# Two fused layers on one core: later sweeps' weights worked out in quads 1 to 12, and the second layer's low halves of weights moved from GpSimd to VectorE

## The chip, the core and the metric

The kernel runs on one core of a Trainium2 chip. Its engines are TensorE (PE in the profile, with its weight loads as PEld), VectorE (DVE), ScalarE (ACT), GpSimd (POOL) and SyncE (SP, which here only issues DMAs). The metric is the device time of one execution in microseconds. The kernel before takes 2681.8 us, the median of three runs (2679.82 to 2686.71).

## The reference, cut to what matters

Two layers follow each other on x of 32 x 128 x 2048 in float32. Layer 0 mixes the 128 channels of each batch by a matrix of its own (a softmax over 8 experts, from a small MLP) and then applies a 2048 x 2048 linear layer whose weight has a low-rank sum added to it. Layer 1 is a grouped convolution of 9 taps and then, on permuted columns, 16 heads of 128 -> 512 -> gelu -> 128. Each layer adds its result to its input.

```
x = x + (einsum('bsd,od->bso', cond(x), W) + bias + einsum('ebsr,eor,e->bso', xa, Bf, coeffs*scales))
t = conv(x)[:, perm]; t = gelu(einsum('bhd,hdm->bhm', t, up)); t = einsum('bhm,hmd->bhd', t, down)
x = x + t[:, unperm]
```

All is float32. The kernel gets that from TensorE's fp32r type by splitting each operand into a high half (a copy rounded to fp32r, `ACT.Copy`) and a low half (the operand minus the high half, one `tensor_tensor` subtract), and by three matmuls: high x high, high x low, low x high.

## The kernel before, in words

**Layer 0.** Two blocks of code follow each other, `layer0_block` and `layer1_block`, with a barrier between them. In the opening of layer 0 the full weight (W plus the low-rank part) is made in 32 tiles, and part of it is stored to `weff_d` in HBM. Then come 32 quads. A quad takes four batches and one quarter of the weight, and does 14 items: 7 products of a Strassen-like scheme for each of two pairs of batches (p = 0, 1). An item is 12 matmuls of 128x512, so a quad is 168 product matmuls (line 478). Eight quads make a sweep, and each sweep uses its own quarter of the weight: `tw_hi` and `tw_lo`, seven matrices of 128x2048 each. Quads 16 to 31 are the final ones: they add the halves of quads 0 to 15, apply the mixing of channels (`mix_v`, 24 more matmuls a quad, line 496), and put the result into x1.

Each engine runs one list of instructions that is written out by `quads(slot, ...)`: for quad q and item t, `slot(q, t)` says what stands there. ScalarE splits off the high half of the left operand three items ahead (`split`, line 611), VectorE the low half (line 952). Four ring buffers hold them, so TensorE has about three items of lead. GpSimd makes the sums of the scheme (lines 789 to 807). In the final quads VectorE also takes results out of PSUM (line 999), splits `v` (line 1011) and applies `take_mixed` (line 1026), and GpSimd issues the accumulating DMAs of the result (line 816).

**The weights of sweeps 1 to 3** need four of the seven matrices as sums of blocks. That is done in 24 pieces, 8 for a sweep. For piece n, SP loads 2 x 256 KB from `weff_d` into `mix` (`load_mix`, line 374) once the store of piece n - 1 has landed, GpSimd adds the blocks to a running sum (lines 309, 311) and makes the four differences (lines 826 to 832), and ScalarE's queue stores `mix` to `t_d` (`store_mix`). There is one `mix` buffer. `mixes(q)` says which pieces a quad does: two in each of quads 1 to 4 (for sweep 1), 9 to 12 (sweep 2) and 17 to 20 (sweep 3). Half a quad before a sweep starts, ScalarE's queue begins to load the seven matrices of 1 MB (`load_tw`), ScalarE splits them (line 701) and VectorE makes their low halves in 28 instructions (line 1031), from item 7 of the sweep's last quad to item 6 of the next.

**Weights of layer 1.** They are 32 chunks of 128x512 (up and down of 16 heads). 16 early chunks go through in layer 0's last quad, two at each of items 6 to 13 (`freed_chunks`): loaded by SP (`load_early`), high half on ScalarE (line 706), low half on GpSimd (`split_early`, line 860). The other 16 go through in layer 1's lead.

**The lead of layer 1** is 20 steps before the first head. In each step u TensorE does the convolution of one unit (9 matmuls, line 1446) and four transposes (line 1458), ScalarE splits the next unit and takes the convolution out, and VectorE makes the low half (line 1599) and takes the transposes (line 1619). SP loads four pieces of each unit (line 88), loads chunks n + 4 and n + 5 after chunks n and n + 1 are split (`load_weights`, line 1266; there are four stage buffers), and after each fourth unit stores four pieces of z (`store_z`, line 1314). The chunks have two of steps 4 to 11 each: high half on ScalarE (line 1512), low half on GpSimd (`split_weights`, line 1377). After the store of the fourth batch GpSimd gathers the first head (line 1371), and TensorE starts `up` (line 1421). From there the two layers' rest, 1080 us, is untouched.

Of the kernel before, what the change touches and what calls it, by code (L numbers as in the profile page):

```python
# [7 lines left out]
ALU = mybir.AluOpType  # L8
# [31 lines left out]
QUADS = 32  # L40
FINAL = QUADS // 2
EARLY = 16
ITEMS = 14
# [69 lines left out]
def sweep(q):  # L113
    return q // 8
# [30 lines left out]
def layer0_block(nc, sh, x, x_t, cond_w, bias_k, cond_t, w0, b0, w1, b1, w2, b2, w_t, bias, lora_a, lora_b, coeffs, scales,  # L145
# [4 lines left out]
    with ExitStack() as ctx:  # L150
# [105 lines left out]
        def freed_chunks(q, t):  # L256

            n = 2 * (ITEMS * (q - QUADS + 1) + t - 6)
            return range(n, n + 2) if 0 <= n < EARLY else ()

# [16 lines left out]
        def mixes(q):  # L277

            return ((q % 8 - 1, 0), (q % 8 - 1, 1)) if 1 <= q % 8 <= 4 and q < 24 else ()

        def mix_count(q):
            return 8 * sweep(q) + 2 * (q % 8 - 1)

# [14 lines left out]

        def sum_piece(eng, engine, q, c):

            n = mix_count(q) + c
            half = HALVES[sweep(q) + 1][0]
            total = sums[half].rearrange("p (b n) -> p b n", b=2)[:, :, c * 256:(c + 1) * 256]
            top, low = mix[:, 0:2, :], mix[:, 2:4, :]
            if q == 1:
                engine.tensor_tensor(total, top, low, ALU.add).then_inc(sums_ready, 1)
            else:
                eng.wait_ge(sums_ready, sums_count(n - 1))
                engine.tensor_tensor(total, total, top, ALU.add).then_inc(sums_ready, 1)
                eng.wait_ge(sums_ready, sums_count(n) - 1)  # L310
                engine.tensor_tensor(total, total, low, ALU.add).then_inc(sums_ready, 1)

        @block.sync
        def _(sp):
# [47 lines left out]

            def load_mix(q, i, c):
                oh, dh = HALVES[sweep(q) + 1]
                n = mix_count(q) + c
                if n == 0:
# [36 lines left out]
            def slot(q, t):  # L403
# [13 lines left out]
                if mixes(q) and t in (0, 7):  # L417
                    load_mix(q, *mixes(q)[t // 7])
# [152 lines left out]
        def _(act):  # L571
# [135 lines left out]

            def store_mix(q, i, c):
                act.wait_ge(t_ready, 16 + 4 * (mix_count(q) + c + 1))
                act.dma_start(t_d[sweep(q), i, :, :, c * 256:(c + 1) * 256], mix[:]).then_inc(mix_out, 16)  # L710

            def slot(q, t):
# [30 lines left out]
                if mixes(q) and t in (6, 12):  # L743
                    store_mix(q, *mixes(q)[t // 12])

# [3 lines left out]
        def _(pool):  # L749
# [67 lines left out]

            def mix_piece(q, c):
                n = mix_count(q) + c
# [3 lines left out]
                sum_piece(pool, nc.gpsimd, q, c)  # L823
                pool.wait_ge(sums_ready, sums_count(n))
# [32 lines left out]

            def split_early(n):
                pool.wait_ge(sh.wsplit_hi, n + 1)
                nc.gpsimd.tensor_tensor(tw_lo[n // 4][:, n % 4, :], w_stage[n % 5], fp32(tw_hi[n // 4][:, n % 4, :]),  # L860
                                        ALU.subtract).then_inc(sh.wsplit_lo, 1)

            def slot(q, t):
# [12 lines left out]
                if mixes(q) and t in (2, 9):  # L876
                    mix_piece(q, t // 9)
# [5 lines left out]
                for n in freed_chunks(q, t):  # L883
                    split_early(n)

# [3 lines left out]
        def _(dve):  # L889
# [123 lines left out]
            def take_mixed(n):  # L1013
# [26 lines left out]
            def slot(q, t):  # L1040
# [12 lines left out]
                for n in range(8 * FINAL, 8 * QUADS):  # L1053
                    if mix_slot(n) + 2 == ITEMS * q + t:
                        take_mixed(n)
                for n in range(1, 4):
                    at = ITEMS * (q - 8 * n + 1) + t - 7
# [11 lines left out]
def layer1_block(nc, sh, x1_d, up, down, perm, ident, z_d, y_d, out):  # L1069

    with ExitStack() as ctx:
# [282 lines left out]
        def _(pool):  # L1354
# [19 lines left out]

            def split_weights(n):
                pool.wait_ge(wsplit_hi, G + n + 1)
                nc.gpsimd.tensor_tensor(chunk(w_lo, n), stage[n % 4], fp32(chunk(w_hi, n)),  # L1377
                                        ALU.subtract).then_inc(wsplit_lo, 1)

            def step(k, h, parity):  # L1380
                if lead(k):
                    for n in chunks_of(k, h):
                        split_weights(n)
                if exists(k, h, 2) and not ahead(k, h):
# [201 lines left out]
        def _(dve):  # L1586
            def split_kernel(g):
# [169 lines left out]
```

## Time and profile before

| | |
|---|---|
| median of 3 runs | 2681.8 us (2679.82 to 2686.71) |
| profiled execution | 2675.54 us, of which its span is 2673.7 us |
| opening of layer 0 | to 117.0 us, the first product matmul |
| quads 0 to 31 | 117.0 to 1507 us |
| end of layer 0 to the first convolution | 1507 to 1526.6 us |
| lead of layer 1 | 1526.6 to 1593.6 us |
| heads of layer 1 | 1593.6 to 2673.7 us |

Quad q starts with the (168 q + 1)-th product matmul. Quads 1 to 7 and 9 to 15 last 38.9 to 39.2 us each, quads 21 to 23 and 25 to 30 last 44.5 to 45.0 us each (they have 24 matmuls more). The others differ: quad 0 lasts 41.8, quad 8 42.5, quad 16 50.9, quads 17 to 20 53.6, 51.1, 51.8 and 50.4, quad 24 52.2, quad 31 48.9 us (to its last product matmul).

### The profile page before, as it was taken

How to read it: one execution, taken by the hardware profiler on the slowest of the kernel's cores; microseconds unless marked ns; L12 is line 12 of the kernel's file. 1: busy time of each engine (PE TensorE's matmuls, PEld its weight loads, DVE VectorE, ACT ScalarE, POOL GpSimd, SP SyncE). 2: the span in 40 equal slices, each digit the busy share in tenths (PEclk: the TensorE clock that was granted, in tenths of full speed). 3: DMA queues.
4: the chain of work that ended last, by engine and by line, in shares of the span. 5: the costliest groups of instructions: out<-in, count | busy, mean ns of one | idle time of the engine just before them, and what ended most of it. 6: DMA issues, size and time to landing. Idle time of an engine off the chain costs nothing. (4 is left out here: it accounts for less than half of the span.)

```text
span 2673.7 us, 38662 instructions
## 1 busy us (share of the span) xinstructions
PE 2558.8 (96%) x11458; PEld 2070.2 (77%) x11458; DVE 2089.7 (78%) x2847; ACT 1143.8 (43%) x1905; POOL 1025.4 (38%) x879
## 2 busy tenths in 40 slices
PE   7899999999999989999999789999999999999997
PEld 6678887888877768878888568888888888888775
DVE  6766767776688788897878658888888888888776
ACT  3233334333342223343333355555555555555563
POOL 4545632674236463344434432222222222222231
PEclk9999999999999999999999899999999999999998
DMA  8887769887776776867676764476767776777686
GB/s 292 285 275 261 259 221 306 267 279 251 237 250 148 179 183 133 224 162 171 138 161 136 157 187 137 138 220 205 231 203 225 212 223 212 222 220 219 191 270 242
DMA packets 437718, 570.38 MB, mean 213 GB/s; under 512 B 38280, under 2 KB 263872, under 8 KB 437504
## 3 DMA queue, kind: packets, MB, share of 16 engines
q1 hardware_dynamic: 329552, 345.68, 42.8%
q0 software_dynamic: 39840, 101.45, 17.3%
q10 hardware_dynamic: 68112, 120.69, 12.8%
q8 instruction: 98, 1.61, 0.3%
q14 instruction: 116, 0.95, 0.1%
HBM read 339.08 MB, written 228.59 MB: 212 GB/s over the span
## 5 line engine op out<-in xcount | busy, mean ns | idle before, releaser
L478 PE MATMUL ps_c<-w_hi,ring_hi 128*128 128x512 f32 x1792 | 711.0, 397 | 6.6 <-DVE ring_lo L952 6.5
L478 PE MATMUL ps_c<-w_hi,ring_lo 128*128 128x512 f32 x1792 | 709.3, 396 | 0.0
L478 PE MATMUL ps_c<-w_lo,ring_hi 128*128 128x512 f32 x1792 | 708.3, 395 | 0.0
L952 DVE TENSOR_TENSOR ring_lo<-raw_n,ring_hi 128x512 fp32r<-128x512 f32 x384 | 447.8, 1169 | 196.2 <-ACT ring_hi L611 184.9
L611 ACT ACTIVATE ring_hi<-raw_n 128x512 fp32r<-128x512 f32 x384 | 243.0, 634 | 758.3 <-PE ps_c L478 503.0
L1403 POOL DMA_INDIRECT y_d<-y_s,idx x128 | 147.1, 1149 | 737.7 <-ACT y_s L1574 680.4
L1541 ACT ACTIVATE kern<-ps_up 128x512 f32<-128x512 f32 x512 | 306.2, 598 | 261.3 <-PE ps_up L1421 233.3
L478 PEld LDWEIGHTS ps_c<-w_hi,ring_hi 128*128 128x128 f32 x1792 | 338.3, 189 | 91.5 <-DVE ring_lo L952 11.6
L478 PEld LDWEIGHTS ps_c<-w_lo,ring_hi 128*128 128x128 f32 x1792 | 338.5, 189 | 79.8 <-issue 0.5
L478 PEld LDWEIGHTS ps_c<-w_hi,ring_lo 128*128 128x128 f32 x1792 | 338.1, 189 | 79.4
L1649 DVE TENSOR_TENSOR g_lo<-kern,g_hi 128x512 fp32r<-128x512 f32 x512 | 354.7, 693 | 40.8 <-ACT g_hi L1545 23.4
L1644 DVE CAST g_hi<-kern 128x512 fp32r<-128x512 f32 x474 | 202.6, 427 | 87.2 <-ACT kern L1541 84.8
L1431 PE MATMUL ps_y<-g_hi,w_hi 128*128 128x512 f32 x512 | 213.5, 417 | 7.0 <-ACT y_s L1574 7.0
L999 DVE TENSOR_TENSOR r_early<-ps_c,r_early 128x512 f32<-128x512 f32 x192 | 131.5, 685 | 100.4 <-PE ps_c L478 99.9
L1431 PE MATMUL ps_y<-g_hi,w_lo 128*128 128x512 f32 x512 | 201.8, 394 | 0.0
L1431 PE MATMUL ps_y<-g_lo,w_hi 128*128 128x512 f32 x512 | 200.9, 392 | 0.0
L1421 PE MATMUL ps_up<-t_hi,w_hi 128*128 128x512 f32 x472 | 187.0, 396 | 7.1 <-DVE t_lo L1608 7.1
L1421 PE MATMUL ps_up<-t_hi,w_lo 128*128 128x512 f32 x472 | 185.8, 394 | 0.0
L1421 PE MATMUL ps_up<-t_lo,w_hi 128*128 128x512 f32 x472 | 184.1, 390 | 0.0
L789 POOL TENSOR_TENSOR s<-raw_n 128x512 f32<-128x512 f32 x64 | 88.8, 1415 | 207.3 <-DMA raw_n<-in_x_t 199.6
L1446 PE MATMUL ps_c<-xp_hi,cw_hi 128*128 128x512 f32 x354 | 142.3, 402 | 17.1 <-DVE xp_lo L1599 17.0
L1558 ACT ACTIVATE z_s<-ps_c,cbias 128x512 f32<-128x512 f32 x118 | 81.1, 688 | 173.5 <-PE ps_c L1446 107.5
(224 smaller groups left out, 4334.2 us busy)
## 6 DMA issues: line engine op xcount, KB each, us to landing
raw_n<-in_x_t SPq DMA_DIRECT2D x128, 512.0 KB, 6.0
u_s<-x_d SPq DMA_DIRECT2D x496, 64.0 KB, 2.2
z_d<-x_s SPq DMA_DIRECT2D x120, 256.0 KB
rear<-y_d SPq DMA_DIRECT2D x112, 256.0 KB
rear<-x_d SPq DMA_DIRECT2D x112, 256.0 KB
out_dram<-results SPq DMA_DIRECT2D x112, 256.0 KB
u_s<-in_x SPq DMA_DIRECT2D x64, 256.0 KB, 5.5
half_d<-r_early ACTq DMA_DIRECT2D x64, 256.0 KB, 4.1
```

The source lines that it names most:

```text
L478: mm = nc.tensor.matmul(bank, a[:, dc, :], w[k][:, dc, :], start=(first and dc == 0 and n == 0), stop=(dc == 3 and n == 2), skip_group_che ...
L611: nc.scalar.activation(ring_hi[g % RING][:].rearrange("p a n -> p (a n)"), ring_raw[p][k], ACT.Copy).then_inc(hi_ready, 1)
L789: nc.gpsimd.tensor_tensor(s1[:, p, :], a21, a22, ALU.add).then_inc(s_ready, 1)
L952: nc.vector.tensor_tensor(ring_lo[g % RING][:].rearrange("p a n -> p (a n)"), ring_raw[p][k], fp32(ring_hi[g % RING][:].rearrange("p a n - ...
L999: nc.vector.tensor_tensor(r_s[p][blk], bank, r_s[p][blk], ALU.add).then_inc(read, 1)
L1403: nc.gpsimd.indirect_dma_start(out=y_d[parity], out_offset=bass.IndirectOffsetOnAxis(ap=idx[:, h:h + 1], axis=0), in_=y_s[j][:], in_offset ...
L1421: mm = nc.tensor.matmul(ps_up[:, mc, :], chunk(w, 2 * h)[:, mc * P:(mc + 1) * P], t, start=(n == 0), stop=(n == 2))
L1431: mm = nc.tensor.matmul(ps_y[:, 0, :], chunk(w, 2 * h + 1)[:, mc * P:(mc + 1) * P], g[:, mc, :], start=(mc == 0 and w is w_hi and g is g_h ...
L1446: mm = nc.tensor.matmul(acc, w[:, 3 * g + tau, :], x[:, tau:tau + Q], start=(tau == 0 and n == 0), stop=(tau == 2 and n == 2))
L1541: nc.scalar.activation(g_s[:, mc, :], ps_up[:, mc, :], ACT.Gelu).then_inc(gelu_done, 1)
L1644: nc.vector.tensor_copy(g_hi[:, mc, :], g_s[:, mc, :]).then_inc(ghi_ready, 1)
L1649: nc.vector.tensor_tensor(g_lo[:, mc, :], g_s[:, mc, :], fp32(g_hi[:, mc, :]), ALU.subtract).then_inc(glo_ready, 1)
```

## The change

`mixes(q)` now gives pieces 2q - 2 and 2q - 1 for each of quads 1 to 12, so that all 24 pieces are done by quad 12, eight quads before the last was done. `EARLY` falls from 16 to 8: eight early chunks pass in layer 0's last quad, one at each of items 6 to 13, and their low halves are made by VectorE. The 24 others pass in the lead of layer 1, two in each of steps 4 to 15, and their low halves are made by VectorE too. The number of instructions of each kind of work is the same; 32 subtractions of 128x512 leave GpSimd for VectorE.

```diff
-EARLY = 16
+EARLY = 8
...
         def freed_chunks(q, t):
 
-            n = 2 * (ITEMS * (q - QUADS + 1) + t - 6)
-            return range(n, n + 2) if 0 <= n < EARLY else ()
+            n = ITEMS * (q - QUADS + 1) + t - 6
+            return range(n, n + 1) if 0 <= n < EARLY else ()
...
         def mixes(q):
 
-            return ((q % 8 - 1, 0), (q % 8 - 1, 1)) if 1 <= q % 8 <= 4 and q < 24 else ()
-
-        def mix_count(q):
-            return 8 * sweep(q) + 2 * (q % 8 - 1)
+            return (2 * q - 2, 2 * q - 1) if 1 <= q <= 12 else ()
...
-            half = HALVES[sweep(q) + 1][0]
+            half, c = HALVES[n // 8 + 1][0], n % 2
...
                 for n in range(EARLY if q == QUADS - 1 else 0):
-                    if t == ((5, 5, 5, 6, 7)[n] if n < 5 else 7 + (n - 4) // 2):
+                    if t == ((5, 5, 5, 6, 7)[n] if n < 5 else 3 + n):
                         load_early(n)
...
+            def split_early(n):
+                dve.wait_ge(sh.wsplit_hi, n + 1)
+                nc.vector.tensor_tensor(tw_lo[n // 4][:, n % 4, :], w_stage[n % 5], fp32(tw_hi[n // 4][:, n % 4, :]),
+                                        ALU.subtract).then_inc(sh.wsplit_lo, 1)
...
+            def split_weights(n):
+                dve.wait_ge(wsplit_hi, G + n + 1)
+                nc.vector.tensor_tensor(chunk(w_lo, n), stage[n % 4], fp32(chunk(w_hi, n)),
+                                        ALU.subtract).then_inc(wsplit_lo, 1)
...
                 if lead(k):
                     split_x(*after(k, h))
+                    for n in chunks_of(k, h):
+                        split_weights(n)
```

Three places in the order of instructions. First GpSimd, from the end of quad 4 through quad 5 into quad 6; `s` and `raw_n` are the sums of the scheme, `kern` and `mix` a piece. Before:

```order
L832 TENSOR_TENSOR mix<-mix 128x256
L789 TENSOR_TENSOR s<-raw_n 128x512 x2
L795 TENSOR_TENSOR raw_n<-raw_n 128x512 x2
L801 TENSOR_TENSOR raw_n<-s,raw_n 128x512 x2
L807 TENSOR_TENSOR raw_n<-raw_n 128x512 x2
L789 TENSOR_TENSOR s<-raw_n 128x512 x2
```

Now:

```order
L827 TENSOR_TENSOR mix<-mix 128x256
L785 TENSOR_TENSOR s<-raw_n 128x512 x2
L791 TENSOR_TENSOR raw_n<-raw_n 128x512 x2
L797 TENSOR_TENSOR raw_n<-s,raw_n 128x512 x2
L803 TENSOR_TENSOR raw_n<-raw_n 128x512 x2
L305 TENSOR_TENSOR kern<-kern,mix 128x2x256
L307 TENSOR_TENSOR kern<-kern,mix 128x2x256
L821 TENSOR_TENSOR mix<-mix 128x256
L823 TENSOR_TENSOR mix<-mix 128x256
L825 TENSOR_TENSOR mix<-mix 128x256
L827 TENSOR_TENSOR mix<-mix 128x256
```

The piece of six instructions stands behind the four pairs of sums, twice in each of quads 5 to 8, and no longer in quads 17 to 20.

Second SP's queue around the start of quad 8, where the sweep changes: `raw_n` are the left operands of quad 8, `u_s` and `x_n` the pieces of x to which the bias is added. Before:

```order
L332 DMA raw_n<-in_x_t 128x1024
L357 DMA u_s<-in_x 128x512
L332 DMA raw_n<-in_x_t 128x1024 x2
L357 DMA x_n<-in_x 128x512 x2
L357 DMA u_s<-in_x 128x512 x2
L346 DMA x_n<-in_bias 128x1024
```

Now:

```order
L370 DMA mix<-weff_d 128x2x256 x2
L328 DMA raw_n<-in_x_t 128x1024
L353 DMA u_s<-in_x 128x512
L328 DMA raw_n<-in_x_t 128x1024
L353 DMA u_s<-in_x 128x512
L328 DMA raw_n<-in_x_t 128x1024 x2
L353 DMA x_n<-in_x 128x512 x2
L370 DMA mix<-weff_d 128x2x256 x2
L353 DMA u_s<-in_x 128x512 x2
L342 DMA x_n<-in_bias 128x1024
```

A pair of `mix` loads stands ahead of quad 8's left operands, and another at quad 8's start, ahead of the loads of x.

Third VectorE in the lead, steps 4 to 6: `g_lo` and `xp_lo` are the low half of a unit, `x_s` and `rear` the transposes taken. Before:

```order
L1599 TENSOR_TENSOR g_lo<-u_s,g_hi 128x514
L1619 COPY x_s<-ps_zt 128x16x32
L1599 TENSOR_TENSOR xp_lo<-u_s,xp_hi 128x514
L1619 COPY rear<-ps_zt 128x16x32
L1599 TENSOR_TENSOR g_lo<-results,g_hi 128x514
```

Now:

```order
L1591 TENSOR_TENSOR g_lo<-u_s,g_hi 128x514
L1583 TENSOR_TENSOR w_lo<-kern,w_hi 128x512 x2
L1611 COPY x_s<-ps_zt 128x16x32
L1591 TENSOR_TENSOR xp_lo<-u_s,xp_hi 128x514
L1583 TENSOR_TENSOR w_lo<-kern,w_hi 128x512 x2
L1611 COPY rear<-ps_zt 128x16x32
L1591 TENSOR_TENSOR g_lo<-results,g_hi 128x514
```

Two subtractions of weights stand between a unit's low half and the taking of the transposes, in 12 steps.

## Rows read from the trace of the kernel before

**Rows 1.** The page, part 1: busy us (share of the span) xinstructions.
```profile
PE 2558.8 (96%) x11458; PEld 2070.2 (77%) x11458; DVE 2089.7 (78%) x2847; ACT 1143.8 (43%) x1905; POOL 1025.4 (38%) x879
```

**Rows 2.** Stretches: quad 6, quad 10, quads 17 to 20, quads 21 and 22.
```profile
core 0: us, PE busy (x) PEld busy (x) DVE busy (x) ACT busy (x) POOL busy (x), PEclk, DMA share, GB/s
353.50:392.40 38.90, 38.90 (x169) 31.55 (x168) 21.13 (x28) 12.50 (x22) 10.31 (x8) 1.00 0.65 202
512.90:551.80 38.90, 38.90 (x169) 31.55 (x168) 28.53 (x29) 12.75 (x22) 26.83 (x21) 1.00 0.83 272
797.70:1004.60 206.90, 186.45 (x770) 148.42 (x769) 173.37 (x182) 54.72 (x92) 122.64 (x113) 0.96 0.71 165
1004.60:1093.60 89.00, 89.00 (x385) 72.10 (x384) 73.39 (x89) 27.39 (x46) 36.90 (x32) 1.00 0.71 148
```

**Rows 3.** Groups of VectorE, quads 17 to 20: count, busy us, mean ns, idle before.
```profile
L952 DVE TENSOR_TENSOR ring_lo<-raw_n,ring_hi 128x512 fp32r<-128x512 f32 x48 | 80.4, 1674 | 8.5 <-ACT ring_hi L611 7.7
```

**Rows 4.** The same of quads 21 and 22.
```profile
L952 DVE TENSOR_TENSOR ring_lo<-raw_n,ring_hi 128x512 fp32r<-128x512 f32 x24 | 30.4, 1269 | 2.0 <-ACT ring_hi L611 1.4
```

**Rows 5.** Timeline in quad 17: start us, us, engine, line, op, tiles [idle before <-releaser].
```profile
804.12 3.77 DVE L952 TENSOR_TENSOR ring_lo<-raw_n,ring_hi 128x512 fp32r<-128x512 f32 x1
...
805.75 1.57 POOL L309 TENSOR_TENSOR kern<-kern,mix 128x512 f32<-128x512 f32 x1
...
809.62 0.50 PE L496 MATMUL ps_v<-v_hi,agg_hi 128*128 128x512 f32 x1 [2.04 <-DVE v_lo L1011]
```

**Rows 6.** Stretches: end of quad 7, start and end of quad 8.
```profile
411.90:431.40 19.50, 19.50 (x85) 15.78 (x84) 13.02 (x19) 9.32 (x13) 4.61 (x4) 1.00 1.03 369
431.40:452.00 20.60, 18.08 (x75) 13.49 (x74) 20.60 (x27) 12.81 (x15) 7.12 (x5) 1.00 0.96 329
452.00:473.90 21.90, 21.90 (x96) 17.75 (x95) 14.89 (x22) 7.07 (x13) 5.56 (x5) 1.00 0.78 261
```

**Rows 7.** DMA issues in quad 2: queue, count, KB each, median us to landing.
```profile
mix<-weff_d SPq DMA_DIRECT2D x4, 256.0 KB, 3.8
...
t_d<-mix ACTq DMA_DIRECT2D x2, 512.0 KB, 3.4
```

**Rows 8.** Waits, 410 to 475 us: engine line <- releaser: total us, times, longest.
```profile
ACT ring_hi L611 <- DMA raw_n<-in_x_t: 12.3, 4, 7.0
```

**Rows 9.** Stretches: quads 30 and 31.
```profile
1413.70:1458.10 44.40, 44.40 (x193) 36.03 (x192) 38.56 (x46) 13.69 (x23) 17.86 (x16) 1.00 0.72 149
1458.10:1507.00 48.90, 44.89 (x192) 35.72 (x191) 43.46 (x44) 22.07 (x37) 30.80 (x27) 1.00 0.67 151
```

**Rows 10.** Groups of VectorE in quad 31.
```profile
L952 DVE TENSOR_TENSOR ring_lo<-raw_n,ring_hi 128x512 fp32r<-128x512 f32 x9 | 15.8, 1758 | 0.8 <-ACT ring_hi L611 0.6
L1011 DVE TENSOR_TENSOR v_lo<-r_early,v_hi 128x512 fp32r<-128x512 f32 x4 | 8.2, 2062 | 0.0
...
L1004 DVE TENSOR_TENSOR agg_lo<-agg,agg_hi 128x512 fp32r<-128x512 f32 x1 | 0.7, 684 | 0.0
```

**Rows 11.** Timeline in quad 31.
```profile
1497.39 6.21 DVE L1011 TENSOR_TENSOR v_lo<-r_early,v_hi 128x512 fp32r<-128x512 f32 x1
...
1503.65 0.50 PE L496 MATMUL ps_v<-v_hi,agg_hi 128*128 128x512 f32 x1 [3.61 <-DVE v_lo L1011]
```

**Rows 12.** SP's own waits, 1525 to 1600 us.
```profile
SPq L1266 <- POOL w_lo L1377: 3.1, 4, 1.6
```

**Rows 13.** Timeline in the lead, 1548 to 1560 us.
```profile
1555.56 1.39 ACT L1512 ACTIVATE w_hi<-kern 128x512 fp32r<-128x512 f32 x2 [4.75 <-DMA kern<-in_up]
```

**Rows 14.** Chain that ended last, in the lead: start us, us, what.
```profile
1568.77 0.42 SPq L88
1569.23 0.42 SPq L88
...
1581.75 0.52 SPq L1314
...
1593.60 1.63 PE ps_up L1421 x3
```

More of the change, by code:

```diff
@@ L297, in sums_count, with sum_piece @@
             return 9 + n if n < 2 else 8 + 2 * n
-        def sum_piece(eng, engine, q, c):
-            n = mix_count(q) + c
-            half = HALVES[sweep(q) + 1][0]
+        def sum_piece(eng, engine, n):
+            half, c = HALVES[n // 8 + 1][0], n % 2
             total = sums[half].rearrange("p (b n) -> p b n", b=2)[:, :, c * 256:(c + 1) * 256]
             top, low = mix[:, 0:2, :], mix[:, 2:4, :]
-            if q == 1:
+            if n < 2:
                 engine.tensor_tensor(total, top, low, ALU.add).then_inc(sums_ready, 1)
@@ L361, in load_r, with load_mix @@
                 sp.dma_start(r_s[p][blk], half_sum(q, p, blk)).then_inc(r_in[p][blk], 16)
-            def load_mix(q, i, c):
-                oh, dh = HALVES[sweep(q) + 1]
-                n = mix_count(q) + c
+            def load_mix(n):
+                oh, dh = HALVES[n // 8 + 1]
+                i, c = n % 8 // 2, n % 2
                 if n == 0:
@@ L417, in slot @@
                 if mixes(q) and t in (0, 7):
-                    load_mix(q, *mixes(q)[t // 7])
+                    load_mix(mixes(q)[t // 7])
                 for n in biased_at(q, t, 0):
@@ L706, in split_early, with store_mix @@
                 nc.scalar.activation(tw_hi[n // 4][:, n % 4, :], w_stage[n % 5], ACT.Copy).then_inc(sh.wsplit_hi, 1)
-            def store_mix(q, i, c):
-                act.wait_ge(t_ready, 16 + 4 * (mix_count(q) + c + 1))
-                act.dma_start(t_d[sweep(q), i, :, :, c * 256:(c + 1) * 256], mix[:]).then_inc(mix_out, 16)
+            def store_mix(n):
+                act.wait_ge(t_ready, 16 + 4 * (n + 1))
+                act.dma_start(t_d[n // 8, n % 8 // 2, :, :, n % 2 * 256:(n % 2 + 1) * 256], mix[:]).then_inc(mix_out, 16)
             def slot(q, t):
@@ L743, in slot @@
                 if mixes(q) and t in (6, 12):
-                    store_mix(q, *mixes(q)[t // 12])
+                    store_mix(mixes(q)[t // 12])
             quads(slot, -3)
@@ L816, in store_mixed, with mix_piece @@
                 pool.dma_start(piece(x1_d, n), res[n % 4], accum_op=ALU.add).then_inc(sh.res_out[n % 4], 16)
-            def mix_piece(q, c):
-                n = mix_count(q) + c
+            def mix_piece(n):
                 pool.wait_ge(mix_in, 32 * (n + 1))
@@ L822, in mix_piece @@
                     pool.wait_ge(twlo_ready, 28)
-                sum_piece(pool, nc.gpsimd, q, c)
+                sum_piece(pool, nc.gpsimd, n)
                 pool.wait_ge(sums_ready, sums_count(n))
@@ L856, in prepare_layer1 @@
                                    conv_w[:, :, kr * GC:(kr + n) * GC]).then_inc(sh.cw_in, 16)
[L858 to L861, printed above, removed]
             def slot(q, t):
@@ L876, in slot @@
                 if mixes(q) and t in (2, 9):
-                    mix_piece(q, t // 9)
+                    mix_piece(mixes(q)[t // 9])
                 for n in range(8 * FINAL, 8 * QUADS):
@@ L882, in slot @@
                     prepare_layer1(q - 24)
-                for n in freed_chunks(q, t):
-                    split_early(n)
             quads(slot, -4)
@@ L1055, in slot @@
                         take_mixed(n)
+                for n in freed_chunks(q, t):
+                    split_early(n)
                 for n in range(1, 4):
@@ L1373, in gather @@
                     in_offset=bass.IndirectOffsetOnAxis(ap=idx[:, h:h + 1], axis=0)).then_inc(t_in[j], 16)
[L1375 to L1378, printed above, removed]
             def step(k, h, parity):
-                if lead(k):
-                    for n in chunks_of(k, h):
-                        split_weights(n)
                 if exists(k, h, 2) and not ahead(k, h):
```

## The prediction

> **What bounds the kernel now.** I read the page's busy times first, and then cut the span into quads, because a share over two unlike layers says little. TensorE is busy 96% of the span, VectorE 78%, GpSimd 38% [rows 1], so time can be won only where TensorE's matmuls stand apart. The view by stretches shows where. In quads 6, 10, 21 and 22 TensorE is busy for the whole stretch; in quads 17 to 20 it is busy for 186.45 of 206.90 us [rows 2]. These four are final quads with the same number of matmuls as quads 21 and 22, which take 89.00 us for two. What they have besides is GpSimd: 122.64 us of work in four quads, against 36.90 us in two [rows 2].
>
> How GpSimd reaches TensorE is seen in VectorE's rows. The subtraction of two operands from SBUF that feeds the ring takes 1269 ns in quads 21 and 22 and 1674 ns in quads 17 to 20 [rows 3, 4]. In the timeline one of them lasts 3.77 us, from 804.12 us on, and spans an addition of a piece on GpSimd that starts at 805.75; TensorE then stands still 2.04 us for a low half of v [rows 5]. VectorE is late by GpSimd's work, and in a final quad it has little room: 73.39 us busy of 89.00 even without pieces [rows 2]. In quad 10 two pieces also run (GpSimd 26.83 us against 10.31 in quad 6), VectorE is busy 28.53 of 38.90 us, and TensorE loses nothing [rows 2]. So a piece costs time in a final quad and none in an early one, unless that quad is itself short of VectorE. One is: at the start of quad 8, where VectorE splits a new sweep's weights, it is busy 20.60 of 20.60 us [rows 6].
>
> **Quads 17 to 20: -28.9 us.** The eight pieces leave. The four quads become like quads 21 and 22: 206.9 - 2 x 89.0 = 28.9 us, or 3.6 us for a piece. Only VectorE's delay goes; what is late next is nothing that shows in quads 21 and 22, whose matmuls stand back to back. The half-speed stretches behind those stalls (the granted clock is 0.96 in the mean there, 1.00 after) are inside the 28.9. I leave quads 16 and 24 as they are, since no piece lay in them.
>
> **Quads 5 to 8: +6.0 us.** The eight pieces arrive in early quads. In 5, 6 and the first half of 7 I cost them at nothing: quad 10 is the row for that, and what hides them is VectorE's 10.4 us of idle time there and TensorE's lead of three items, which is 3 x 12 x 0.232 = 8.4 us (38.9 us over 168 matmuls is 0.232). The second piece of quad 7 and the first of quad 8 meet the change of sweep. There two things are full. The DMA engines show a share of 1.03 at 369 GB/s from 411.9 to 431.4 us, and 0.96 after it [rows 6]; ScalarE already waits for left operands around it, 12.3 us in four times, the longest 7.0 [rows 8]. VectorE has no idle time at the start of quad 8, and TensorE is busy 18.08 of these 20.60 us [rows 6].
> A piece moves 2 x 256 KB in and 512 KB out, 1 MB [rows 7]. Of this the load of the piece at quad 7's item 7 and part of the store before it, about 0.9 MB, go ahead of quad 8's left operands: 0.9 MB at 369 GB/s is 2.4 us later for operands whose slack is already used up. To it comes the first piece of quad 8, beside a full VectorE, at the 3.6 us of the final quads, together 6.0 us. The ends: nothing, if it is hidden as in quad 10; and 6.2 + 5.4 = 11.6 us if VectorE stands still for all of GpSimd's work in a piece ((122.64 - 2 x 36.90) / 8 = 6.1 us, taken as 6.2 with the gaps) and 2 MB are in the way. SP's queue counts here too: it waits at quad 8's start until the store of the piece before has landed, and the loads of x for the bias are behind that wait. In the trace these loads wait for other stores anyway, so I add nothing, but it is inside the upper end.
> A VectorE subtraction of 3.77 us spans a whole GpSimd addition of 1.57 us [rows 5]. The Trainium skill (SBUF — State Buffer, "Who interferes with whom") says that a VectorE instruction with two SBUF inputs contends with a GpSimd instruction that reads SBUF, and that the one which starts first holds the ports for its whole length while the other fully blocks. By that rule the piece in quad 8 costs about its whole 6.2 us and the sum below is 2.6 us less of a gain; by quads 17 to 20 it costs 3.6, because instructions that read PSUM slip between, and I go by these. Full blocking is in the second rival.
>
> **Quad 31: -4.5 us.** Quad 31 takes 48.9 us and quad 30 44.4, with the same matmuls [rows 9]. In it GpSimd makes 16 low halves (30.80 us busy against 17.86), and VectorE's instructions swell: four subtractions of v take 2062 ns each, one of them 6.21 us, and TensorE waits 3.61 us for it [rows 10, 11]. Now GpSimd makes none. VectorE gets eight more, at the 0.68 us of an undisturbed one [rows 10], 5.5 us. It gives back more than that: nine ring subtractions at 1758 instead of 1269 ns [rows 4, 10] and four of v at 2062 instead of 684 are 4.4 + 5.5 = 9.9 us. So it would be busy 43.5 - 9.9 + 5.5 = 39.1 of 44.4 us, as in quad 30 (38.56). Each new one stands last in its item, behind which is the next item's take out of PSUM; its high half was made by ScalarE earlier in the same item. Ends: -4.5 and, if the eight fall on TensorE's waits for v, -4.5 + 5.5 = +1.0.
>
> **The lead: +2.4 us.** The chain that ended last runs here over SP's queue: from 1568.77 us it is one issue after another, 0.46 us apart, to the store of z at 1581.75, its landing, the gather and the first `up` at 1593.60 [rows 14]. SP, not TensorE, sets the lead's end. Eight more chunks are eight more issues ahead of that store: 8 x 0.46 = 3.7 us. Against it, SP waited 3.1 us in four times for GpSimd's low halves, 1.6 us the longest [rows 12]; VectorE makes one in 0.68 us, and I count 1.3 us of the 3.1 as won, the rest being the wait for ScalarE's half and for VectorE's own queue. Behind the two new subtractions in VectorE's queue stands the taking of the transposes, and for that TensorE and the stores of z wait. A step's VectorE work is then 4 x 0.68 = 2.7 us beside TensorE's 9 x 0.232 = 2.1 us and four transposes, so the two are about level; both are less than SP's four loads, two chunks and one z store in the mean, 7 x 0.46 = 3.2 us or more. Ends: 3.7 - 3.1 = +0.6, and 3.7 + 4.8 = +8.5 if one more wait for a chunk like the one at 1555.56 us comes about [rows 13].
> The chain's rows say that issuing is the bound here. The Trainium skill (DMA: Bandwidth & Descriptors, "Issuing engines are not separate DMA queues") calls the sequencer's time to start a DMA usually small relative to the DMA itself. By that rule this term would be -1.3 instead of +2.4, which belongs to the first rival.
>
> **The sum.** -28.9 + 6.0 - 4.5 + 2.4 = -25.0 us. Against the profiled execution's 2675.5 us that is 2650.5. The median of the timed runs is 6.3 us above this execution, and I take the change as the same there: 2681.8 - 25.0 = 2656.8, rounded to 2657 us.
>
> **The rivals.**
> First, everything that arrives is hidden. Quads 7 and 8 behave like 10, and the lead costs only its lower end: -28.9 - 4.5 + 0.6 = -32.8 us, 2649 us. For it speaks quad 10; against it the DMA share of 1.03 and the saturated VectorE [rows 6]. Chance 0.17.
> Second, the change of sweep clogs. VectorE's two-input work stands for the whole of a piece, 2 MB queue ahead of left operands and weights, and the lead gets one more wait for a chunk: -28.9 - 4.5 + 11.6 + 8.5 = -13.3 us, 2668.5 us. What speaks for it is one long subtraction, the full stretch and one late chunk [rows 5, 6, 13]; against it, that quad 8 recovers in its second half (VectorE 14.89 of 21.90). Chance 0.17.
> Third, slower: VectorE's queue now holds each chunk's wait in front of the transposes. A chunk that is late (4.75 us at ScalarE, once in the trace [rows 13]) would stall every one of the 12 steps: 12 x 4.75 = 57 us on the sum, 2657 + 57 = 2714 us. It decides where SP issues a chunk so late that it lands after its step has come, and makes the kernel slower from 6 such waits on. Against it: ScalarE already stood in the same wait before, and it came once. Chance 0.03.
> Fourth, the change doesn't do what it says in quads 17 to 20, as their loss comes from the start of the final quads and not from the pieces: then 28.9 stays, +3.9 us, 2686 us. Against it, quad 21 is clean at once. Chance 0.02.
> My forecast has the remaining 0.61.
>
> **How the numbers follow.** The likeliest case gives 2657. The range goes from 2645 (the first rival and 4 us for the runs' spread) to 2669 (the second). Of this kernel's time 0.3%, 8 us, can be told from no change. Forecast and the first two rivals are all faster by more: 0.95, of which I keep 0.01 back for mishaps. Same 0.03, slower 0.03.
>
> **What would show it.** Right: quads 17 to 20 at 44.5 us each with no wait of TensorE for v; the ring subtraction there near 1270 ns; quads 5 and 6 at 38.9; quad 8 some 6 us longer than its 42.5, with longer waits of ScalarE for `raw_n`; quad 31 near 44.5; the first `up` 69 us after the first convolution instead of 67. Wrong: a quad 17 that keeps its waits, or stalls in quads 5 and 6, or a lead in which ScalarE waits for `kern` at most steps.

## The result, and the profile after

The changed kernel takes 2664.2 us in the median of 5 runs (2661.0 to 2666.3), the kernel before 2680.9 us in 5 runs on the same chip (2677.6 to 2686.7). The ratio is 0.9935, with a 95% interval from 0.9920 to 0.9949: 16.8 us less, where 25 were forecast. The time lies inside the range (2645 to 2669), in the part of it that was kept for a clogged change of sweep.

The view by stretches of the changed kernel, cut into quad 6, 7, 8, 9, quads 17 to 20 and quad 31 (us, then busy us and count of each engine, the granted clock, the DMA engines' share and GB/s):

```profile
352.00:390.90 38.90, 38.90 (x170) 31.54 (x169) 28.55 (x29) 13.05 (x23) 26.93 (x22) 1.00 0.82 273
390.90:434.30 43.40, 39.29 (x170) 31.46 (x168) 27.52 (x36) 16.62 (x24) 21.09 (x18) 0.99 0.96 325
434.30:486.00 51.70, 44.58 (x168) 33.89 (x168) 41.02 (x49) 20.21 (x27) 28.38 (x23) 0.91 0.87 274
486.00:525.70 39.70, 39.21 (x168) 31.49 (x169) 26.40 (x31) 13.23 (x24) 23.79 (x20) 1.00 0.84 270
810.90:989.50 178.60, 178.31 (x770) 144.17 (x769) 148.46 (x181) 54.77 (x92) 74.06 (x65) 1.00 0.70 148
1445.60:1489.90 44.30, 44.30 (x193) 35.86 (x192) 36.49 (x52) 16.70 (x29) 10.30 (x11) 1.00 0.60 119
```

In quads 17 to 20 TensorE now stands still for 0.3 us (20.5 before [rows 2]), in quad 31 not at all [rows 9], and the granted clock is 1.00 in both. Quad 6 takes GpSimd's work without loss. Quads 7 to 9 take 134.8 us; before they took 39.0 + 42.5 + 39.0 = 120.5. That is 14.3 us given back, of 33 won. Part by part, in the two profiled executions:

| part | forecast | measured |
|---|---|---|
| quads 17 to 20 | -28.9 | 178.6 - 206.9 = -28.3 |
| quads 5 to 9 | +6.0 | +14.3, none of it in 5 and 6 |
| quad 31 | -4.5 | 44.3 - 48.9 = -4.6 |
| lead, first convolution to first `up` | +2.4 | 70.1 - 67.0 = +3.1 |

The sum is -15.5 us; the two profiled executions differ by 14.6. The remaining stretches (start to first product, quad 24, the heads of layer 1) differ by up to 2 us each with either sign, and by more among the experiments, where nothing in them was changed: the start is 115.3 to 118.6 us, quad 24 51.8 to 54.8, the heads from the first `up` to the end 1079.6 to 1084.8.

So one thing needs an explanation: quads 7 and 8. SP's queue, in the timeline of the changed kernel (start us, us, engine, line, operation, tiles):

```profile
407.34 0.33 SPq L353 DMA_DIRECT2D x_n<-in_x  x1
418.46 1.18 SPq L370 DMA_DIRECT2D mix<-weff_d  x2
419.70 0.59 SPq L328 DMA_DIRECT2D raw_n<-in_x_t  x1
```

For 11 us SP issues nothing: it stands before the load of piece 13, which waits until the store of piece 12 has landed, and the loads of quad 8's left operands (`raw_n<-in_x_t`) are behind it. In the kernel before the first of them was issued at 413.62, 21.2 us after the start of quad 7; here it is 28.7 us after. GpSimd, ScalarE and TensorE in the same view:

```profile
426.70 1.29 POOL L305 TENSOR_TENSOR kern<-kern,mix 128x512 f32<-128x512 f32 x1 [19.52 <-DMA mix<-weff_d]
...
432.54 2.95 POOL L785 TENSOR_TENSOR s<-raw_n 128x512 f32<-128x512 f32 x2
```
```profile
433.00 0.63 ACT L607 ACTIVATE ring_hi<-raw_n 128x512 fp32r<-128x512 f32 x1 [10.13 <-DMA raw_n<-in_x_t]
```
```profile
434.41 0.80 PE L474 MATMUL ps_c<-w_hi,ring_hi 128*128 128x512 f32 x1 [4.22 <-DVE ring_lo L940]
```

There are two lines of waiting here, not one. SP stands before the piece's load, and GpSimd stands before the piece, with quad 8's sums (`s<-raw_n`) behind it in its own order: they start 41.5 us after quad 7's start instead of 28.5. And the stall has a tail. The stretches around it:

```profile
430.10:433.50 3.40, 0.09 (x1) 0.00 (x0) 0.00 (x0) 0.50 (x1) 3.17 (x5) 1.00 1.01 365
433.50:440.30 6.80, 5.49 (x12) 3.84 (x12) 6.64 (x5) 4.16 (x6) 6.80 (x5) 0.51 0.91 275
...
460.80:464.20 3.40, 3.40 (x10) 2.64 (x9) 3.40 (x6) 0.00 (x0) 0.73 (x1) 0.52 0.70 242
```

Behind the 4.22 us in which TensorE did nothing, and again behind a wait of 1.75 us at 459.85, its granted clock is at the lower of its two levels, 1.2 GHz: 10.2 us in all, of which half is lost. That agrees with the busy time: TensorE is busy 123.1 us in quads 7 to 9 for the same matmuls that took 118.0 before. So 5.1 of the 14.3 us are clock, and 9.2 are standing still.

### The profile page after: what moved, and what is told of

The parts are those of the page before. It is cut to its first block and busy times, and to the rows that moved or that the text cites. A ratio compares the mean times of both kernels' runs of the same rounds, so it can differ in the third digit from the quotient of the medians.

```text
span 2659.2 us, 38654 instructions
## 1 busy us (share of the span) xinstructions
PE 2558.8 (96%) x11458; PEld 2069.5 (78%) x11458; DVE 2081.9 (78%) x2879; ACT 1142.6 (43%) x1905; POOL 986.3 (37%) x847
## 3 DMA queue, kind: packets, MB, share of 16 engines
q0 software_dynamic: 39840, 101.45, 17.4%
q10 hardware_dynamic: 68112, 120.69, 12.9%
## 5 line engine op out<-in xcount | busy, mean ns | idle before, releaser
L940 DVE TENSOR_TENSOR ring_lo<-raw_n,ring_hi 128x512 fp32r<-128x512 f32 x384 | 427.0, 1115 | 194.3 <-ACT ring_hi L607 189.2
L1366 POOL DMA_INDIRECT u_s<-z_d,idx x128 | 130.8, 1022 | 107.9 <-issue 105.1
```

The costliest lines, as they stand in the source:

```text
L940: nc.vector.tensor_tensor(ring_lo[g % RING][:].rearrange("p a n -> p (a n)"), ring_raw[p][k], fp32(ring_hi[g % RING][:].rearrange("p a n - ...
L1366: nc.gpsimd.indirect_dma_start(out=t_s[j], out_offset=None, in_=z_d[parity], in_offset=bass.IndirectOffsetOnAxis(ap=idx[:, h:h + 1], axis= ...
```

## The experiments

Quads 7 to 9 are told here in one number, the time from quad 7's first product to quad 10's. In the profile of the kernel before it is 120.5 us, in that of the changed kernel 134.8. All 24 pieces are stored and used as in the changed kernel unless something else is said.

**Which half of the change does what.** The change has two separate parts, so each was run alone. The early chunks and the lead alone:

```diff
-EARLY = 16
+EARLY = 8
 (low halves and the lead's chunks to VectorE; mixes(q) as before)
```

> The kernel before with only the second half of the change: 8 early weight chunks with low halves on VectorE, 24 split in the second layer's lead; the weight pieces stay in quads 1 to 4, 9 to 12 and 17 to 20. Theory: quad 31 falls from 48.9 to about 44.3 us and the lead (first convolution product to first up product) rises from 67.0 to about 70.1 us, quads 7 to 9 stay at 120.5 and quads 17 to 20 at 206.9; the time is 1 to 2 us less than before (ratio about 0.9995, within 0.3%). Rival: quad 31 gains only because GpSimd's pieces had moved out of quads 17 to 20 (less work left over on VectorE), then quad 31 stays above 47 us and the time is slower by 1 to 3 us.

Ratio 0.9991 (0.9978 to 1.0005). Quads 7 to 9 take 121.6 us, the lead 70.7, and quads 17 to 20 and 31:

```profile
799.80:1008.20 208.40, 189.45 (x770) 150.77 (x769) 173.67 (x182) 54.72 (x92) 122.65 (x115) 0.93 0.72 164
1463.40:1507.70 44.30, 44.30 (x193) 35.87 (x192) 36.63 (x52) 16.79 (x29) 10.48 (x11) 1.00 0.58 119
```

Quad 31's gain belongs to this half alone, and the lead takes nearly all of it back. The pieces alone:

```diff
-            return ((q % 8 - 1, 0), (q % 8 - 1, 1)) if 1 <= q % 8 <= 4 and q < 24 else ()
+            return ((q, 0), (q, 1)) if 1 <= q <= 12 else ()
```

> The kernel before with only the first half of the change: the 24 weight pieces stand in quads 1 to 12, while the early chunks stay 16 with low halves on GpSimd. Theory: quads 17 to 20 take about 178.7 us instead of 206.9 (-28.2), quads 7 to 9 take about 134.8 instead of 120.5 (+14.3), quad 31 stays 48.9 and the lead 67.0; the sum is -14 us, about 2667 us, ratio about 0.995. Rival: part of the loss in quads 7 to 9 comes from elsewhere in the change (its opening is 1.8 us earlier), then quads 7 to 9 are below 130 us and the ratio is below 0.993.

Ratio 0.9952 (0.9936 to 0.9967), 12.9 us less. Quads 17 to 20 take 178.1 us and quads 7 to 9 137.9; quad 31 stays at 48.5 and the lead is 65.6. The rival is out: the loss comes with the pieces. The two halves add up to 2.4 + 12.9 = 15.3 us, beside 17.4 of the whole (ratio 0.9935), within the intervals.

**The pieces out of quads 7 and 8.**

```diff
-            return (2 * q - 2, 2 * q - 1) if 1 <= q <= 12 else ()
+            first = 2 * q - 2 if 1 <= q <= 6 else 2 * q - 6 if 9 <= q <= 14 else None
+            return () if first is None else (first, first + 1)
```

> The changed kernel with one thing different: GpSimd's weight pieces 0 to 23 stand in quads 1 to 6 and 9 to 14 instead of 1 to 12, so quads 7 and 8 hold none. Theory (the head-of-line wait of SyncE's queue behind the store of piece 12, and DMA traffic of pieces 12 to 15 against the raw and residual loads of quads 8 and 9): quads 7 to 9 take 120.5 us together as in the kernel before (they are 134.8 in the changed kernel), quads 13 and 14 stay within 1 us of 39 each, and the time is 2664 - 14 = about 2650 us, ratio to the kernel before about 0.989. Rival A (the loss belongs to this many pieces in succession, not to quads 7 and 8): a loss of 5 us or more appears in quads 9 to 14 and the total stays within 4 us of 2664. Rival B (VectorE late because of port sharing with GpSimd anywhere at the turn of a sweep): quads 7 and 8 recover but quads 15 and 16, whose sweep turns again, lose 5 us or more.

2648.8 us, ratio 0.9883 (0.9865 to 0.9901). Quads 7, 8 and 9:

```profile
393.70:433.30 39.60, 39.28 (x170) 31.46 (x168) 26.73 (x36) 16.64 (x23) 10.48 (x7) 1.00 0.92 309
433.30:476.90 43.60, 39.97 (x168) 31.26 (x169) 36.74 (x50) 20.62 (x28) 13.90 (x10) 1.00 0.87 287
476.90:515.90 39.00, 39.00 (x170) 31.57 (x169) 29.01 (x30) 12.76 (x22) 25.65 (x20) 1.00 0.81 266
```

122.2 us, clock 1.00, and quads 10 to 16 are within 0.8 us of before (194.7, 40.0 and 50.1 us; 194.7, 39.2 and 50.9). Both rivals are out: it is these two quads, and the work costs nothing elsewhere, not even in quads 13 and 14.

**Which resource of the pieces in quads 7 and 8.** What follows takes one thing at a time away from pieces 12 to 15 or adds one. First their transfers:

```diff
+                    w = 16 if 12 <= n < 16 else P
-                    sp.dma_start(mix[:, 2 * e:2 * e + 2, :], ...
+                    sp.dma_start(mix[0:w, 2 * e:2 * e + 2, :], ...
 (the same for the store; pieces 8 to 11 store a second 448 KB)
```

> The changed kernel with the loads and stores of weight pieces 12 to 15 (quads 7 and 8) cut to 16 of 128 partitions, 64 KB instead of 512 KB each; GpSimd's arithmetic on them is whole, so the effective weights of those pieces are wrong in the output. Theory (transfers and the queue wait behind them): quads 7 to 9 fall from 134.8 us to 121 to 124 us. Rival (GpSimd's arithmetic of pieces 12 to 15 slows VectorE, 3 to 4 us of sums beside each quad, or GpSimd finishes its sums too late): quads 7 to 9 stay above 130 us. Other quads stay as in the changed kernel; the pieces 8 to 11 store 448 KB more each, so quads 5 and 6 may gain a us or two.

130.7 us: neither forecast. The added stores made piece 12 late (its load 402.1 instead of 393.8 us), and SP waited all the same, to 422.06. So it was run again without them:

```diff
-                    src = t_d[n - 1, ...
+                    src = t_d[0 if n == 2 else n - 1, ...
 (loads and stores of pieces 12 to 15 with w = 16 partitions, nothing added)
```

> The first run with small transfers was blurred: it stored 448 KB more beside each of pieces 8 to 11, which made piece 12 late (its load at 402.1 instead of 393.8) and held SyncE until 422.1. Here loads and stores of pieces 12 to 15 cover 16 of 128 partitions and nothing is added before them (the third sweep reads the second's operands, wrong in value). If traffic and the waits on it make the whole loss but for VectorE's slower instructions beside GpSimd (about 3 us by the run with tiny arithmetic), quads 7 to 9 take 122 to 125 us; if GpSimd's arithmetic and its order are more than that, above 127 us.

128.8 us, above 127: traffic and VectorE's slowing are not the whole. SP's queue, the store of piece 12, the wait of TensorE, and the stretch behind it:

```profile
415.52 1.18 SPq L371 DMA_DIRECT2D mix<-weff_d  x2
416.76 0.57 SPq L328 DMA_DIRECT2D raw_n<-in_x_t  x1
```
```profile
DMA to landing us min/median/max: 7.3/7.3/7.3
```
```profile
432.95 0.79 PE L475 MATMUL ps_c<-w_hi,ring_hi 128*128 128x512 f32 x1 [3.10 <-DVE ring_lo L942]
```
```profile
432.00:438.80 6.80, 5.85 (x14) 4.59 (x15) 6.80 (x7) 3.81 (x6) 4.90 (x4) 0.50 0.97 267
```

A store of 64 KB needs 7.3 us here, and the one of 512 KB in the changed kernel 9.9. The same store of 512 KB took 10.3, 8.9 and 8.5 us in three other runs with all of its bytes, and stores of 64 KB took 7.3, 6.7 and, once issued later, 4.9 us. An eighth of the bytes takes away about a third of the wait; the rest would then be other transfers of the full stretch, which no run shows by itself. The stall of 3.10 us is there, and the half-speed stretch with it.

Then the wait behind the store, with all traffic kept:

```diff
+                w = 16 if 12 <= n < 16 else P      (stores only)
+                if 12 <= n < 16:
+                    act.dma_start(dump_d[n - 12], w_t[0:P, 0:HALF]).then_inc(dump_out, 16)
```

> The changed kernel where the stores of pieces 12 to 15 cover 16 of 128 partitions, so that SyncE's wait for them ends early, and each is followed by a copy of 512 KB within HBM that nothing waits for, so that the traffic stays; GpSimd's arithmetic is whole. Output: the third sweep reads the second sweep's operands, so its products are wrong in value. If the wait behind the store is the main cause, quads 7 to 9 take 121 to 125 us; if the traffic is, 130 to 136 us, with ScalarE still 7 us or more waiting for raw_n near the start of quad 8.

135.5 us. It did not free the wait: SP issued the load of piece 13 at 416.62, 25.7 us after quad 7's start, against 27.4 in the changed kernel, since the small store landed only 6.7 us after its issue. The run tells nothing between the theories.

GpSimd's arithmetic:

```diff
+            w = 1 if 12 <= n < 16 else 256
-            top, low = mix[:, 0:2, :], mix[:, 2:4, :]
+            top, low = mix[:, 0:2, 0:w], mix[:, 2:4, 0:w]
 (the same for the four differences)
```

> The changed kernel with GpSimd's arithmetic on weight pieces 12 to 15 cut from 256 or 512 columns to 1 or 2; loads and stores stay whole, so the traffic is the same and the effective weights of those pieces are wrong. Theory after the run with small transfers, where SyncE still waited 41 us for the stores of pieces (the wait is the whole chain load, 8 us of arithmetic, store, and not the transfer time alone): the store of piece 12 is issued about 7 us earlier, SyncE's wait before piece 13 ends about 7 us earlier, and quads 7 to 9 take 121 to 127 us instead of 134.8. Rival (traffic): 131 us or more.

131.7 us. The theory's number is missed: SP's wait ended at 419.25, 27.8 us after quad 7's start, as in the changed kernel. GpSimd was done with the piece at 402.8 us, and ScalarE issued its store at 409.0, 17.5 us after quad 7's start, as in the changed kernel: ScalarE's own place in its program decides that, not GpSimd. What is won is VectorE's: quad 8 has it busy 35.13 us instead of 41.02.

```profile
435.70:483.50 47.80, 43.00 (x169) 32.92 (x169) 35.13 (x49) 19.71 (x27) 14.88 (x21) 0.95 0.91 299
```

SP's order alone. The loads of pieces 13 and 15, with their wait, go to GpSimd's queue:

```diff
-                if mixes(q) and t in (0, 7):
+                if mixes(q) and t in (0, 7) and mixes(q)[t // 7] not in (13, 15):
 (mix_piece: GpSimd waits for the store before and issues both halves of the load)
```

> The changed kernel with the loads of weight pieces 13 and 15 (the second one of quads 7 and 8) issued by GpSimd from its own queue instead of by SyncE; the wait for the store of the piece before goes with them. Nothing is computed otherwise and the traffic is the same. Theory (SyncE's in-order queue stands behind that store, so the raw loads of the next quad start 28.8 us after quad 7's start instead of about 21): SyncE issues the raw loads from about 21 us on, quad 7 takes 39 to 40 and quad 8 43 to 46, quads 7 to 9 together 121 to 126 us instead of 134.8. Rival A (GpSimd itself is what is late: its sums for quad 8 stand behind piece 13 in its own order and start at 432.5): it is still there, so quads 7 to 9 stay above 131 us though the raw loads come early. Rival B (the traffic, 369 GB/s with the DMA engines full): the raw loads issue early but land as late as before, quads 7 to 9 stay above 131 us, and ScalarE still waits about 10 us for raw_n.

135.8 us, above the 131 of both rivals. SP, GpSimd and the waits around the middle of quad 8, and the quad:

```profile
414.25 0.33 SPq L328 DMA_DIRECT2D raw_n<-in_x_t  x1
```
```profile
437.29 3.44 POOL L785 TENSOR_TENSOR s<-raw_n 128x512 f32<-128x512 f32 x2
```
```profile
444.69 0.50 PE L474 MATMUL ps_c<-w_hi,ring_hi 128*128 128x512 f32 x1 [3.69 <-DVE ring_lo L949]
445.81 0.63 ACT L607 ACTIVATE ring_hi<-raw_n 128x512 fp32r<-128x512 f32 x1 [3.15 <-POOL raw_n L797]
```
```profile
433.40:485.90 52.50, 43.44 (x169) 33.38 (x169) 43.10 (x49) 19.74 (x27) 30.06 (x24) 0.93 0.83 277
```

The left operands' loads start on time again (21.1 us), quad 7 takes 40.3 us instead of 43.4, and everything comes back in quads 8 and 9 (52.5 and 43.0): GpSimd's sums now start 44.2 us after quad 7's start, and ScalarE waits for `raw_n` from GpSimd (8.5 us in three times, none in the changed kernel). That is rival A. Rival B doesn't fit at the start of quad 8, where ScalarE now waits 2.55 us for a load instead of 10.13. One wait of 9.72 us for a load is left, before 484.43, at quad 8's end, but the run with the traffic alone, told below, has it too (9.92 us). The theory that SP's wait is the cause falls with this run. It is one of two doors to the same stall.

The traffic alone. To the kernel without pieces in these quads eight copies of 512 KB within HBM are added, at the pieces' places, and nothing waits for them:

```diff
+                if q in (7, 8) and t in (0, 6, 7, 12):
+                    act.dma_start(dump_d[...], w_t[0:P, 0:HALF]).then_inc(dump_out, 16)
```

> The kernel with the pieces in quads 1 to 6 and 9 to 14 (quads 7 to 9 took 122.2 and 121.2 us in its two profiles), with one thing added: in quads 7 and 8 ScalarE issues four copies of 512 KB each from one place in HBM to another that nothing waits for, at the places where pieces 12 to 15 were loaded and stored. So these quads have the pieces' traffic without their arithmetic and without any wait. If the traffic is the main cause of the loss (ScalarE waited about 10 us for raw_n in every variant so far, early issue or not), quads 7 to 9 take 129 to 135 us. If it is the order in SyncE's and GpSimd's queues, they stay at 121 to 124 us.

```profile
432.90:479.40 46.50, 40.83 (x168) 31.00 (x168) 35.10 (x50) 20.38 (x28) 12.51 (x9) 1.00 0.95 318
```

125.8 us, 4 more than without (122.2 and 121.2 us), between the two forecasts. No half-speed stretch.

**One piece in each of the two quads.**

```diff
+            if q in (7, 8):
+                return (q + 5,)
```

> The changed kernel with one piece instead of two in quads 7 and 8 (12 and 13, each as the first piece of its quad, whose load and GpSimd work lie ahead of the next quad's raw loads and sums), and pieces 14 to 23 in quads 9 to 13. If the loss comes from what stands in front of the raw loads and sums (the second piece of a quad), quads 7 to 9 take 121 to 124 us and the time is that of the kernel without pieces in quads 7 and 8, ratio 0.988. If it follows the amount (traffic and GpSimd's time), about half of the 12 to 14 us stays: 127 to 129 us, ratio about 0.991.

2651.2 us, ratio 0.9895 (0.9867 to 0.9924). The left operands' loads start 21.2 us and the sums 28.7 us after quad 7's start, both as before.

```profile
434.10:481.40 47.30, 40.71 (x169) 31.20 (x170) 39.77 (x49) 20.82 (x28) 20.41 (x15) 1.00 0.85 288
```

126.5 us, between the forecasts and nearer the one by amount: a third to two fifths of the loss stay with half of the pieces. The clock stays at 1.00.

**The lead.** The last 20 chunk loads from ScalarE's queue instead of SP's:

```diff
-                            load_weights(n + 4)         (SP, behind the stores of z)
+                                act.wait_ge(wsplit_lo, G + n + 1)
+                                act.dma_start(stage[n % 4], weight_chunk(up, down, n + 4)) ...
```

> The changed kernel with the last 20 weight loads of the second layer's lead issued from ScalarE's queue, right behind the z activation of the step, instead of from SyncE's, so SyncE issues 4 x loads a step and the stores of z. Theory (SyncE's 0.46 us an issue, and its waits for the low halves, set the pace of the lead): the lead (first convolution product to first up product) falls from 70.1 to 64 to 67 us, all else stays, and the time is 3 to 6 us below 2664. Rival (VectorE's and ScalarE's own splits set the pace, ScalarE now with 20 more issues and a wait for VectorE in its order): the lead stays at 70 or rises to 75 us.

Ratio 0.9926 (0.9903 to 0.9948), which can't be told from the changed kernel's 0.9935. The lead takes 68.2 us, in the next run 67.9: 2 us less, not 3 to 6. And the ten profiles in which the lead stands as in the changed kernel have 68.6 to 71.8 us, so even the 2 us lie only just outside their spread. The two profiles with the lead as before have 67.0 and 65.6. Quads 7 to 9 took 135.8 us, so the changed kernel's arrangement there has three profiles, 134.8, 135.8 and 137.9; differences of 2 us between single profiles mean little.

**Both together.**

> The pieces in quads 1 to 6 and 9 to 14 and the lead's last 20 weight loads from ScalarE's queue together. If both act alone as expected, 2649 less 3 to 6 us: 2643 to 2646 us, ratio to the kernel before 0.9865 or so; if the lead's change brings nothing, 2649 us again (0.988).

2646.7 us, ratio 0.9877 (0.9857 to 0.9898): quads 7 to 9 121.2 us, the lead 67.9. By the ratio it is 1.6 us better than the kernel without pieces in quads 7 and 8, which the intervals don't tell apart. These two are the best versions found, and either beats the changed kernel, whose interval lies wholly above theirs.

## Why the prediction was right, and where it was not

The time after quad 7's start of the first load of left operands and of GpSimd's first sum, beside quads 7 to 9 (one profile each, in the order of the last column):

| kernel | first load | first sum | clock in quad 8 | quads 7 to 9 |
|---|---|---|---|---|
| before | 21.2 | 28.5 | 1.00 | 120.5 |
| none in 7 and 8 | 21.2 | 29.1 | 1.00 | 122.2 |
| traffic alone | 21.2 | 28.8 | 1.00 | 125.8 |
| one piece each | 21.2 | 28.7 | 1.00 | 126.5 |
| small transfers | 26.1 | 37.9 | 0.94 | 128.8 |
| small transfers, first run | 28.4 | 39.6 | 0.95 | 130.7 |
| tiny arithmetic | 29.0 | 37.8 | 0.95 | 131.7 |
| changed kernel | 28.7 | 41.5 | 0.91 | 134.8 |
| small stores with copies | 26.9 | 42.5 | 0.96 | 135.5 |
| loads by GpSimd | 21.2 | 44.2 | 0.93 | 135.8 |
| changed kernel, lead's loads from ScalarE | 27.9 | 41.8 | 0.91 | 135.8 |
| pieces alone | 27.9 | 42.2 | 0.93 | 137.9 |

- **Quads 17 to 20, quad 31.** Right, to 0.6 and 0.1 us, and the first by its mechanism: with the pieces alone moved, these four quads take 178.1 us. The ring subtraction in quads 17 to 20 fell to the value read beside it [rows 4]:

```profile
L940 DVE TENSOR_TENSOR ring_lo<-raw_n,ring_hi 128x512 fp32r<-128x512 f32 x48 | 61.1, 1272 | 5.4 <-ACT ring_hi L607 4.4
```

  It was right because a neighbouring stretch of the same kernel had the same matmuls without the pieces. VectorE is busy 36.49 us in quad 31, less than the 39.1 worked out.
- **Quads 5 and 6.** Right: no loss.
- **Quads 7 and 8.** The place and the kind were right, the size was not: +14.3 instead of +6.0, over the upper end of 11.6. Four steps of this term failed. First, the sentence "In the trace these loads wait for other stores anyway, so I add nothing" spoke of the loads of x for the bias at quad 8's start; the wait that mattered is the one before piece 13, and behind it are the left operands' loads, 7.5 us later than before. Second, the sum charged the piece by its bytes, "0.9 MB at 369 GB/s is 2.4 us", but a store an eighth as large still took 7.3 us of 9.9 to land. Third, GpSimd's order was not read at all: piece 13 stands ahead of quad 8's sums, which started 13 us later. Fourth, no half-speed stretch was charged, though for quads 17 to 20 it was known to be inside the number: 5.1 us.
- **The time in its range.** The direction came from the largest term, which was right. That the time lies below 2669 in spite of a term over its upper end is partly luck: the upper end had +8.5 in it for the lead, which took +3.1 and left the room.
- **What is shown of the cause.** With the pieces out of these quads the loss is gone. With all their traffic and no wait it is about 4 us. With the first piece of each quad and its traffic it is 4 to 5 us. The second piece, ahead of the loads and the sums, makes up the rest, some 8 us; its own traffic and its arithmetic beside VectorE are in them too. By single profiles small transfers take away 6.0 us and tiny arithmetic 3.1, of four pieces each. Taking away SP's place alone brings nothing, since GpSimd's remains. In the table the time goes with the first sum and not with the first load, but in no run are the sums late and all else as before. GpSimd's late sums alone were not tried without the rest, so how the 8 us divide between the two queues, the traffic and VectorE's slowing stays open.
- **VectorE's slowing** beside GpSimd: 41.02 us busy in quad 8 with two pieces, 36.74 without: 4.3 us for 28.38 - 13.90 = 14.5 us more of GpSimd. So choosing a price below full blocking of all of GpSimd's time was right. Below it are VectorE and GpSimd at the start of quad 8, where both have work without a pause:

```profile
435.96 3.45 DVE L1024 TENSOR_TENSOR w_lo<-w_lo,w_hi 128x512 fp32r<-128x512 f32 x2
439.34 1.75 DVE L940 TENSOR_TENSOR ring_lo<-raw_n,ring_hi 128x512 fp32r<-128x512 f32 x1
```
```profile
435.45 3.41 POOL L791 TENSOR_TENSOR raw_n<-raw_n 128x512 f32<-128x512 f32 x2
438.83 1.71 POOL L797 TENSOR_TENSOR raw_n<-s,raw_n 128x512 f32<-128x512 f32 x1
```

  A subtraction that takes 0.68 us by itself takes 1.75, and an addition of 1.30 takes 1.7: they go in turns, and each of VectorE's loses about 1.1 us to one of GpSimd's. The Trainium skill (SBUF — State Buffer, "Who interferes with whom") calls the shared ports an exclusive lock, under which the later one is fully blocked, and these rows agree with it. What the rule doesn't give is how often the two meet, and 4.3 of 14.5 us is what came of it here.
- **The lead.** +3.1 for +2.4. The size was right; that SP's issues make it is not shown. With 20 issues taken from SP the lead is 2 us shorter at the most, and it doesn't get below 67.9, while SP's waits for low halves fell from 3.1 to 1.4 us, more than was counted. In the changed kernel the chain that ended last runs over a chunk's load and VectorE's queue before it reaches SP's last issues:

```profile
1555.74 4.47 DMA kern<-in_down
1560.24 0.64 ACT w_hi L1499
1560.94 0.57 issue
1561.51 0.68 DVE rear L1611
1562.20 0.60 DVE xp_lo L1591
1563.32 0.68 DVE w_lo L1583
1564.00 0.60 DVE rear L1611
1564.60 0.61 DVE g_lo L1591
1566.05 0.42 SPq L88
```

  The low half (`w_lo`) is now one link of it. The third rival did not come about: ScalarE's longest wait for a chunk is 4.1 us, the one before was 4.75 [rows 13]. Its sign did, however: ScalarE waits for `kern` in seven of the 12 steps. But the nine waits are 1.4 us in the mean, where the rival had 4.75, and 12.6 us together (the two rows below; 7.7 in the kernel before). With the loads from ScalarE's queue they are 4.4 us:

```profile
ACT w_hi L1499 <- DMA kern<-in_up: 9.6, 4, 4.1
...
ACT w_hi L1499 <- DMA kern<-in_down: 3.0, 5, 1.4
```

  There the chain shows what comes next:

```profile
1552.04 6.21 DMA kern<-in_down
1558.28 0.64 ACT w_hi L1495
1558.94 0.70 DVE w_lo L1584
1559.66 4.87 DMA kern<-in_down
```

  A chunk's load, its high half, its low half, and only then the load of the fourth chunk after it, since there are four stage buffers. The chain goes round this way from 1537.40 to 1564.56 us, in 7.1 to 7.6 us a turn, and a turn is two steps. That points at the four stage buffers and the loads' 4.9 to 6.2 us, and not at the queue that issues; no run changed them.
- **The rivals.** The second, a clogged change of sweep at 2668.5 us, lies 4 us from the measured time and the forecast 7. Its picture of quads 7 and 8 was the better one (11.6 for 14.3), its +8.5 in the lead came out as +3.1. It was given 0.17; the row that spoke for more was the DMA share of 1.03 [rows 6], together with the order of SP's and GpSimd's programs. The first rival and the fourth fall with quads 7 to 9 and 17 to 20.

## What to carry to other kernels

When work is moved into a stretch, read for each in-order queue what stands behind its first instruction, not how long the work takes: a piece that waits for its own store stops every load and every sum that comes after it in the program. Price a transfer in a full stretch by the time that other transfers of that stretch take to land, not by its bytes alone: the store of a piece took 3.4 us in quad 2 [rows 7] and 8.5 to 10.3 here. And to a stall of TensorE add what the trace shows behind such stalls for the clock, here half of a 6.8 us stretch behind 4.22 us.

## What the runs showed of the hardware that was not expected

Stores of 64 KB took 4.9, 6.7 and 7.3 us to land, and those of 512 KB 8.5 to 10.3, near the middle of quad 7, where the DMA engines are full. And the granted clock: in all eight runs with two pieces in quads 7 and 8 it fell to its lower level around the end of TensorE's longest wait near the start of quad 8, of 3.10 to 5.74 us, and in four of them again at waits of 1.75 to 3.10 us. But it stayed at its higher level behind a wait of 2.73 us at the start of quad 9 in the run with tiny arithmetic, and behind one of 2.23 us there in the changed kernel, so the length of a wait doesn't decide it by itself. In the runs with at most one piece in quad 8 it stayed at its higher level there.
